# A fused block with a pruned gate: squares in other columns, a rewritten prologue, one rounding and the flag sums moved

## What is computed

```python
x = x + 0.5 * ffn(layernorm(x), A, B, Wr)      # step 1
x = x + attn(layernorm(x), w_gate, w_up, w_down)  # step 2
x = x + 0.5 * ffn(layernorm(x), A, B, Wr)      # step 3, the same weights

def ffn(x):       # 64 experts of rank 16, the best 16 with softmax weights
    scores = x @ Wr.T
    top_vals, top_idx = top_k(scores, 16); gates = softmax(top_vals)
    h = einsum('nd,krd->nkr', x, A)
    return einsum('nkr,kdr->nd', h * G[:, :, None], B) * 2

def attn(x):      # I = 1376; the 688 gate values of least magnitude are zeroed
    s = silu(x @ w_gate.T)
    s[rows, top_k(-abs(s), 688)] = 0
    return (s * (x @ w_up.T)) @ w_down.T
```

## Time and profile before

| | us |
|---|---|
| median of 3 runs | 831.62 |
| lowest, highest | 831.41, 834.43 |
| the profiled execution | 832.65 |
| its span on the core | 830.8 |
| PE busy | 725.8 (87%) |
| DVE, ACT, POOL busy | 480.1, 359.8, 212.9 |

### The profile page before, as it was taken

One profiled execution on the slowest core, in us unless ns is written; L12 is line 12 of the kernel. 1 busy time (PEld: TensorE's weight loads), 2 busy tenths in 40 slices (PEclk: granted clock), 3 DMA queues, 4 the chain that ended last, 5 costly groups with the idle time before them and its releaser, 6 DMA issues.

```text
span 830.8 us, 10394 instructions
## 1 busy us (share of the span) xinstructions
PE 725.8 (87%) x3674; PEld 337.4 (41%) x3679; DVE 480.1 (58%) x1015; ACT 359.8 (43%) x447; POOL 212.9 (26%) x618
## 2 busy tenths in 40 slices
PE   4676779759999999999999999999999996989684
PEld 1223334324454545444444444444445442434231
DVE  6656647446666576665747475665666553544631
ACT  5454655425253534435352625352535343446110
POOL 4013030314132323223140504141323222223100
PEclk9997889879999999999999999999999997999898
DMA  8429412315152424334243333251414140403221
GB/s 327 119 89 197 112 27 39 60 13 99 32 95 49 99 51 82 68 68 83 61 83 68 63 81 69 54 83 37 89 38 99 26 86 13 86 19 81 52 59 38
DMA packets 170524, 62.29 MB, mean 75 GB/s; under 512 B 163632, under 2 KB 163632, under 8 KB 170464
## 3 DMA queue, kind: packets, MB, share of 16 engines
q1 hardware_dynamic: 167952, 51.01, 31.3%
q0 software_dynamic: 2512, 10.55, 4.0%
HBM read 16.97 MB, written 4.19 MB: 25 GB/s over the span
## 4 chain that ended last, share of the span: by engine, by line
DVE 32%; POOL 19%; issue 18%; ACT 13%; PE 12%; DMA 3%; DVEq 1%; SPq 1%; POOLq 0%; ACTq 0%
ACT signs L719 9%; POOL small L411 5%; POOL small L409 4%; PE ps L480 4%; PE ps L482 4%; PE ps L481 4%; DVE mem L1007 3%; DVE small L1009 3%; POOL small L408 3%; DVE mem L1026 3%; DVE mem L987 3%; DVE mem L1087 3%; DVE stats L908 3%; POOL small L407 2%; ACT mem L737 2%
## 5 line engine op out<-in xcount | busy, mean ns | idle before, releaser
L719 ACT ACTIVATE signs<-mem,small 128x1376 bf16<-128x1376 f32 x112 | 161.4, 1441 | 144.5 <-POOL small L411 125.6
L480 PE MATMUL ps<-w_b_hi,pt_hi 128*128 128x512 f16 x256 | 97.7, 382 | 21.1 <-issue 21.1
L480 PE MATMUL ps<-w_a_hi,xt_f 128*128 128x512 f16 x256 | 101.9, 398 | 5.2 <-DVE routed L957 3.4
L481 PE MATMUL ps<-w_a_hi,xt_f 128*128 128x512 f16 x256 | 101.4, 396 | 0.0
L482 PE MATMUL ps<-w_a_lo,xt_f 128*128 128x512 f16 x256 | 101.3, 396 | 0.0
L389 POOL TENSOR_SCALAR rvar<-mv 128x1 f32<-128x1 f32 x48 | 11.4, 237 | 351.1 <-DVE mv L909 350.1
L481 PE MATMUL ps<-w_b_hi,pt_lo 128*128 128x512 f16 x256 | 97.7, 382 | 0.0
L482 PE MATMUL ps<-w_b_lo,pt_hi 128*128 128x512 f16 x256 | 97.5, 381 | 0.0
L967 DVE TENSOR_TENSOR p_lo<-routed,p_hi 128x1024 f16<-128x1024 f32 x32 | 39.2, 1225 | 85.5 <-ACT p_hi L714 75.8
L480 PE MATMUL ps<-w_u_hi,xt 128*128 128x512 f16 (+1 forms) x192 | 70.3, 366 | 6.7 <-DVE mem L987 6.7
L480 PE MATMUL ps<-w_g_hi,xt 128*128 128x512 f16 (+1 forms) x192 | 70.9, 369 | 3.9 <-issue 3.9
(11 more groups left out here) (130 smaller groups left out, 1218.6 us busy)
## 6 DMA issues: line engine op xcount, KB each, us to landing
x<-x SPq DMA_DIRECT2D x14, 256.0 KB, 3.0
out<-x SPq DMA_DIRECT2D x14, 256.0 KB, 2.4
mem<-w_g POOLq DMA_DIRECT2D x4, 688.0 KB, 8.2
mem<-w_u POOLq DMA_DIRECT2D x4, 688.0 KB, 7.4
mem<-w_d POOLq DMA_DIRECT2D x5, 512.0 KB, 12.0
mem<-w_a SPq DMA_DIRECT2D x4, 512.0 KB, 6.2
mem<-w_b POOLq DMA_DIRECT2D x4, 512.0 KB, 6.5
pt_hi<-p_hi SPq DMA_TRANSPOSE x32, 3.2
```

The costliest lines, as they stand in the source:

```text
L480: pe.matmul(dst, x_hi, w_hi, start=start, stop=False)
L481: pe.matmul(dst, x_lo, w_hi, start=False, stop=False)
L719: act.activation(signs[:, :], mags[t % 2], ACT.Sign, bias=thr, scale=-1.0, accum_out=bal).then_inc(counted, 1)
```

## The change

Five things are changed.

1. `squares` gives each matrix a place of its own, in weight columns that are filled later: a in w_u_hi, b in w_u_lo, g in w_d_hi, u in w_d_lo, d in the staging memory of u. `square` no longer waits for `norm_summed`; d's first square waits until u's lo is made. The zeroing of w_d's last rows moves behind silu(0).
2. The prologue's orders on PE, ACT, DVE, POOL and SP are rewritten; in the `experts` with `norms_of` the sums of squares now come before w_a's product, not in the middle of it.
3. In the steady tile, ScalarE's `p_to_hi(number[3, d])` moves from behind count 5 to behind count 4.
4. The flags' sum goes into bank DOWN. It waits for `x2_ready` (add_down of the tile before has read that bank), and `down`, not the next scores, waits for `flag_read`. In the rounds d = 11 and 12 it moves behind `gates`.
5. Pieces 2 and 3 of w_a are issued by GpSimd, pieces 0 and 1 by SyncE.

```diff
         def squares(m, n):
-            one = xt_2[1].rearrange("p c t -> p (c t)") if m is MD else signs[:, :]
-            two = keep[:, :]
-            return [one, two][(pieces_before(m) + n) % 2].bitcast(BF16)
+            c, k, rows = m.pieces[n]
+            place = {"r": signs[:, :], "a": hi["u"], "b": lo["u"], "g": hi["d"], "u": lo["d"],
+                     "d": mem[:, 0:2 * IPAD]}[m.name]
...
             load_x(0)
-            load_w(MR)
-            load_w(MA)
+            load_w(MR, 1)
+            load_w(MA, 2)
             load_x(1)
             load_x(2)
+            load_x(3)
             turn_x(1, 2)
...
@@ gpsimd
+            load_w(MA, 2)
+            load_w(MA, 3)
             rstd(1, 0)
...
-            searches(0, 0, 1, 2)
+            searches(0, 0, 1)
             rstd(2, 2)
-            searches(0, 3, 4, 5)
+            searches(0, 2, 3, 4, 5)
...
@@ experts on PE
                 mm.then_inc(scored, 1)
+                if norms_of is not None:
+                    norms(norms_of)
                 if k:
                     pe.wait_ge(routed_ready, k)
...
-                        if o == 0 and norms_of is not None:
-                            norms(norms_of)
...
@@ down on PE
+                pe.wait_ge(flag_read, t + 1)
                 pe.wait_ge(vt_hi_loaded, 16 * (t + 1))
...
-            def sum_flags(t, k):
-                pe.wait_ge(scores_read, k + 1)
+            def sum_flags(t):
+                if t:
+                    pe.wait_ge(x2_ready, t)
                 pe.wait_ge(flag_ready, t + 1)
-                pe.matmul(bank(SCORE, 1, KE), ones[:, :], flag[:, 0:1], start=True, stop=True
+                pe.matmul(bank(DOWN, 1), ones[:, :], flag[:, 0:1], start=True, stop=True
...
@@ tile on PE
-                sum_flags(d + 1, number[1, d + LEAD] - 1)
+                sum_flags(d + 1)
                 gates(d + 2)
-                pe.wait_ge(flag_read, d + 2)
                 experts(1, d + LEAD)
...
@@ prologue on PE
             experts(1, 1, norms_of=MB)
-            pe.wait_ge(scale_made, 3)
             experts(1, 2, norms_of=MG)
             combine(1, 0, fresh=True)
             experts(1, 3)
             combine(1, 1)
+            pe.wait_ge(scale_made, 4)
             norms(MU)
-            pe.wait_ge(scale_made, 4)
             gates(0, fresh=True)
+            combine(1, 2)
+            experts(1, 4)
+            ups(0, fresh=True)
             pe.wait_ge(scale_made, 5)
-            norms(MD, 0, 2)
-            combine(1, 2)
-            norms(MD, 2, 4)
-            ups(0, fresh=True)
-            norms(MD, 4, 6)
-            experts(1, 4)
+            norms(MD)
             combine(1, 3)
             gates(1)
-            pe.wait_ge(scale_made, 6)
-            sum_flags(0, 4)
             combine(1, 4)
+            pe.wait_ge(scale_made, 6)
+            sum_flags(0)
             ups(1)
...
@@ rounds d = 11 and 12 on PE
                 combine(3, d - 1)
-                sum_flags(d + 1, number[3, d] - 1)
                 gates(d + 2)
-                pe.wait_ge(flag_read, d + 2)
+                sum_flags(d + 1)
                 experts(3, d)
...
@@ square on ACT
                 act.wait_ge(w_loaded[m.name][n], 16)
-                if turn >= 2:
-                    act.wait_ge(norm_summed, turn - 1)
+                if m is MD and n == 0:
+                    wait_low(act, MU, len(MU.pieces) - 1)
...
@@ tile on ACT
                 exps(number[3, d])
-                counts(d + 2, 4, 5)
+                count(d + 2, 4)
                 p_to_hi(number[3, d])
-                count(d + 2, 6)
+                counts(d + 2, 5, 6)
...
@@ prologue on DVE, a part
             apply_route(0)
+            make_scale(MB)
+            make_unscale(unscale_f, "ab", -24)
+            choose(1)
             p_to_lo(0)
             norm_stats(1, 3)
-            choose(1)
-            make_scale(MB)
-            make_unscale(unscale_f, "ab", -24)
             route(1)
             apply_route(1)
             norm_apply(1, 3)
-            split_all(MB)
             make_scale(MG)
             make_unscale(unscale_g, "g", 38)
+            split_lo(MB, 0)
+            x_to_lo(1, 3)
+            split_lo(MB, 1)
+            choose(2)
+            split_lo(MB, 2)
+            split_lo(MB, 3)
             p_to_lo(1)
-            x_to_lo(1, 3)
-            choose(2)
             route(2)
             apply_route(2)
```

More of the change, by code:

```diff
@@ L267, in load_x, with load_w @@
                 sp.dma_start(slot(t), x[t * P:(t + 1) * P, :]).then_inc(x_loaded[t % SLOTS], 16)
-            def load_w(m):
-                for n, (c, k, rows) in enumerate(m.pieces):
+            def load_w(m, end):
+                for n, (c, k, rows) in list(enumerate(m.pieces))[:end]:
                     src = dram[m.name][c * P:c * P + (k - 1) * P + rows, :]
@@ L658, in _ @@
             combine(3, NT - 4)
-            sum_flags(NT - 2, number[3, NT - 3] - 1)
+            sum_flags(NT - 2)
             ups(NT - 1)
-            pe.wait_ge(flag_read, NT - 1)
             experts(3, NT - 3)
@@ L664, in _ @@
             combine(3, NT - 3)
-            sum_flags(NT - 1, number[3, NT - 2] - 1)
-            pe.wait_ge(flag_read, NT)
+            sum_flags(NT - 1)
             experts(3, NT - 2)
@@ L800, in _ @@
             tanh(0)
-            square(MD, 2)
-            square(MD, 3)
             x_to_hi(2, 1)
+            square(MD, 0)
+            square(MD, 1)
             magnitude(0)
             count(0, 0)
+            square(MD, 2)
+            exps(4)
+            count(0, 1)
+            square(MD, 3)
+            count(0, 2)
+            p_to_hi(4)
             square(MD, 4)
-            count(0, 1)
+            count(0, 3)
             square(MD, 5)
-            x_to_hi(1, 4)
-            count(0, 2)
-            count(0, 3)
-            exps(4)
             count(0, 4)
-            p_to_hi(4)
             x_to_hi(2, 2)
@@ L1075, in check @@
                 dve.wait_ge(flag_summed, t + 1)
-                dve.tensor_copy(flagged, bank(SCORE, 1, KE)).then_inc(flag_read, 1)
+                dve.tensor_copy(flagged, bank(DOWN, 1)).then_inc(flag_read, 1)
                 dve.wait_ge(flag_read, t + 1)
@@ L1138, in _ @@
             turned_to_lo(1)
+            split_lo(MA, 0)
             norm_stats(1, 2)
-            split_all(MA)
+            for n in range(1, len(MA.pieces)):
+                split_lo(MA, n)
             norm_apply(1, 2)
@@ L1183, in _ @@
             silu(0)
-            wait_low(dve, MU, len(MU.pieces) - 1)
-            link(dve.memset(masked[:, I:IPAD], 0.0))
+            if LAST < P:
+                link(dve.memset(hi["d"][LAST:P, IC - 1, :], 0.0))
+                link(dve.memset(lo["d"][LAST:P, IC - 1, :], 0.0))
             add_ffn(1, 2)
             norm_stats(2, 2)
-            x_to_lo(1, 4)
-            gated(0)
-            make_scale(MD)
-            make_unscale(unscale_m, "gud", -83)
             choose(4)
@@ L1198, in _ @@
             x_to_lo(2, 2)
+            make_scale(MD)
+            make_unscale(unscale_m, "gud", -83)
+            link(dve.memset(masked[:, I:IPAD], 0.0))
+            gated(0)
             add_ffn(1, 3)
@@ L1201, in _ @@
             norm_apply(1, 5)
+            split_lo(MD, 0)
             select(0)
             mask(0)
-            split_all(MD)
+            for n in range(1, len(MD.pieces)):
+                split_lo(MD, n)
             x_to_lo(1, 5)
```

71 lines of the change are left out of this document (34 added, 37 removed).

## The result

| | before | after |
|---|---|---|
| median | 832.74 us (4 runs, 831.41 to 834.43) | 809.74 us (4 runs, 807.73 to 811.34) |
| profiled execution | 832.65 | 807.73 |
| its span | 830.8 | 805.9 |
| PE busy | 725.8 | 718.3 |

The ratio is 0.972, with a 95% interval of 0.969 to 0.975. The forecast was 806 in a range of 795 to 815, and -25.2 us between the profiled executions, where -24.9 were measured. The medians differ by 23.0.

A forecast was written before the change was run, and what follows sets the result against it. The search, not PE, was taken to set the steady period; waits on loads and squares delayed the prologue. Terms -27.1 + 2.2 + 0 - 0.3 = -25.2 from 832.65 gave 807.4, as a median 806.4, range 795 to 815.

The forecast's parts named there:

- VectorE's new order laid with old durations: Prologue up to silu(1): 121.1 for 148.22, so -27.1 us, with bounds of -31 and -21.
- The flag in bank DOWN: PE's flag sum must wait for add_down: +2.2 us once, in the first tile, and 0 in a steady tile.
- the rounding: Steady tile, p_hi of step 3 behind count 4: count 5 comes 1.0 later, the last at the old time; 0.
- Half of w_a by GpSimd: Start of the prologue: bandwidth sets w_a's landing, so issuing from two engines is worth 0, from -0.5 to +0.5 us.
- p_lo(2)'s transpose: Prologue: caught by w_d's load, it lands 15.1 us after d's first issue, up to 3 more; 73.5 taken.
- The ending: Rounds 11 and 12 and the last tiles, with the flag sum behind the gates: -0.3 us, from -1.5 to +2.
- A: Rival, steady search: p_lo begins slightly later, the threshold correction stays short, ten tiles gain 1.0 each: 796 us; chance 0.12.
- B: Rival, prologue: w_d's load also catches the transposes xt_0 and p_hi(2), +4 to +7, 812 us; chance 0.12.
- C: Rival, steady tiles: PE's new wait for add_down lengthens each tile, 14 more tiles cost 31, 837 us; chance 0.03.
- D: Rival, prologue: something unseen (low clock, GpSimd's port) bounds the first search, half the gain, 819 us; chance 0.07.

The follow-up runs named there:

- e5: The changed kernel with part 4 undone, the flags' sum back in bank SCORE with its old waits: 807.70 us.
- e6: The changed kernel with part 3 undone, p_hi of step 3 behind count 5 again: 810.04 us.
- e1: The changed kernel with all four pieces of w_a issued by SyncE again: 809.15 us.
- e11: The changed kernel with the edits of e3, e5 and e1 together: 788.68 us.
- e12: e11 with the edit of e8 added, w_u and w_d held back: 786.99 us.
- e2: The changed kernel, with VectorE's p_lo of step 3 waiting until GpSimd's threshold correction of that round is done: 799.64 us.
- e3: e2 with p_lo of step 1 also waiting for the threshold correction it meets, and in the two shorter rounds too: 792.10 us.
- e10: The changed kernel with the flags' sum ahead of the gates again in rounds 11 and 12: 807.34 us.
- e8: The changed kernel, with GpSimd issuing w_u only after p_lo(1)'s transpose has landed and w_d only after p_lo(2)'s: 808.80 us.

## Why the prediction was right, point by point

| | forecast | after |
|---|---|---|
| first `routed`, start to end | 26.0 to 27.3 | 27.57 to 28.80 |
| second, third, fourth | 34.0, 46.8, 61.0 | 35.48, 48.11, 62.39 |
| p_lo(3) | 73.5 | 73.14 |
| silu(0), select(0) | 81.6, 108.9 | 81.14, 108.89 |
| silu(1) | 121.1 | 120.99 |
| flag sum of tile 1, against silu(1) | +2.2 | +2.3 |
| steady period | 43.9 to 44.2 | 43.9, 44.2 |
| idle time ahead of the flags' sum | 1.4 | 1.17 |
| ending, from the raising of flag 12 | -0.3 | +0.1 |

*Right in kind and size:* VectorE's new order laid with old durations holds to 0.2 us from one `routed` to the next, and the search of tile 0 to 0.5. The flag in bank DOWN (e5) and the rounding (e6) cost what was said.

*Right by two errors that cancel:* the first `routed` is 1.5 us later than before, and the fourth 1.4 later than forecast. The step that failed is "Half of w_a by GpSimd", bounded by -0.5 and +0.5; at the first `routed` it costs 1.2 (e1, e11, e12). The bounds rested on the bytes, whose last piece is indeed only 0.4 later, and not on the order of arrival: ScalarE wants the pieces one by one. The Trainium skill ("DMA: Bandwidth & Descriptors", "Issuing engines are not separate DMA queues") says that the transfers of several issuing engines interleave and that only issue time is saved. The landings agree with both; that the term is 0 for a reader of single pieces doesn't follow from it. Against this error stands p_lo(2)'s transpose. d's load starts at 59.34 and not at 57.5, but the 15.1 us from its first issue to the landing, and the up to 3 more, were too long: p_lo(3) begins 13.8 later. silu(0) follows the landing of p_lo(2) by 8.1 us in after, e1, e2, e3, e5, e6, e10 and e11, whatever came before, so a late start and a short hold could cancel. That they did so to 0.5 us is luck.

*Not seen:* w_u's load, forecast at about 45, catches p_lo(1)'s transpose, which is issued 0.9 us behind its first transfer (9.9 us, 2.70 of PE's idle time at 57.45). I had checked x(3), xt_0 and p_hi(2) against the loads, not this one. It had room here. Nor did p_hi(2) pass untouched: issued 0.45 us ahead of d's load it took 5.3 us for the 3.1 assumed, and nothing waited for it.

*The ending* came out at +0.1 for -0.3, but not by the forecast's terms. check(12) waits 6.1 us more for the flags' sum than before, where 1.9 were said; flag 13 is 2.2 later for it (44.50 us behind flag 12 for 42.35), and all of that is given back by the end.

*The median:* 806.4 took 1.03 us off because the profiled execution of before lay that far above its median. The profiled execution of after lies 2.0 us below its median instead. The two make up 3.0 of the 3.3 us by which the median misses the forecast.

*PE's work of a tile* was put at 42.7, the period less the idle time. It is 42.51 (e3). Where PE stands idle once in a tile, that costs 0.2 us beyond what the view shows as idle, and as much for a short stop as for a long one: 43.91 less 1.17 (after), 43.25 less 0.51 and 42.95 less 0.21 (e2) all leave 42.74. One reading is off as well: the earlier trace rows's stretch has nine idle times of 1.2 to 1.6 us and one of 0.85, not ten.

*The rivals:* A was rightly given a small chance for this kernel and its mechanism is confirmed. It was worth 10 us, as said (e2). B didn't come about, since xt_0 and p_hi(2) were issued ahead of d's load; what it would have cost, no run shows. C is refuted by 197.55:637.98, D by the table.

*Still open:* why the same load takes longer in one execution than in another. silu(0) stands 53.0 us behind the first `routed` in e3 and 54.3 in e2, on one chip and with the same code up to there; that is p_lo(2)'s transpose, which took 10.1 and 11.8 us beside w_d's load.

## What to carry to other kernels

Where engines wait for one another in a ring and a short instruction takes 1.38 us instead of 0.34 in each turn, look for the long instruction that starts some hundredths ahead of it, and make the long one wait: that was worth 17 us here, in both kernels, for a few lines. Squares, sums and other scratch belong where no reader holds them, as in weight columns that are filled later; before an order is rewritten, that alone gave 15 us. A bound by bandwidth is not enough for a load whose pieces have a serial reader: ask in which order the pieces land. And where an engine's stream holds back a load, look at what stands behind the load in that stream (e8).
